# One image's latent scores earlier in TensorE's order, local values and gates sharing a bank, gates taken from the queries

## The reference

```
mod = silu(c) @ wmod                       # six rows of 128 per image: sa, ca, ga, sb, cb, gb
h   = layernorm(x) * (1 + ca) + sa
Q, K, V = h @ wq, h @ wk, h @ wv           # 16 heads of 8
local   = softmax(Q K / sqrt(8), windows of 32 tokens and the 32 before them) V
GQ, GK, GV = h @ wgq, pool(h @ wgk), pool(h @ wgv)     # 8 latent heads of 8, 64 latents, 4 tokens each
rem     = softmax(GQ GK / sqrt(8), causal over latents) GV @ r_out_w
gl, gr  = sigmoid(sum_d Q * gate_local_w), sigmoid(sum_d Q * gate_remote_w)   # one number per head
x = x + ga * ((gl * local + gr * rem) @ w_out)
h = layernorm(x) * (1 + cb) + sb
g = mean_s(relu(h @ gate_w1.T + gate_b1) @ gate_w2.T + gate_b2)               # 8 experts
x = x + gb * (gelu(h @ mW1.T + mb1) @ mW2.T + mb2)     # mW1 = W1 + sum_e g_e TW1_e, and so on
```

## Time and profile before

| what | value |
|---|---|
| median of three runs | 748.62 us |
| profiled execution | 748.97 us, span 747.20 us, granted TensorE clock 0.979 |
| busy share of the span | PE 86%, VectorE 72%, ScalarE 52%, GpSimd 39% |
| share of the chain that ended last | PE 42%, VectorE 26%, ScalarE 15%, issue 14% |
| one pass of the loop, `rden` to `rden` | 16.35 us, 28 passes |
| tanh of the gates in a pass | starts at 329.13, 0.58 us |

### The profile page before, as it was taken

The page is one execution under the profiler, slowest core; times in us unless marked ns, Lnnn a source line. Parts: engine busy times, 40 slices in busy tenths (PEclk is TensorE's granted clock), DMA queues, the critical chain, the costliest instruction groups (busy, mean ns, idle before and its releaser), DMA issues.

```text
span 747.2 us, 24120 instructions
## 1 busy us (share of the span) xinstructions
PE 645.6 (86%) x8822; PEld 506.4 (68%) x8822; DVE 538.1 (72%) x1241; ACT 384.9 (52%) x910; POOL 294.9 (39%) x415
## 2 busy tenths in 40 slices
PE   5588888788888878888887888888779999999998
PEld 3366666566666656666665666666558999898996
DVE  5568788888878888887888888788755546273552
ACT  2256655666665566666555666655543223423233
POOL 2256555455555545555554555555530000000000
PEclk9699999999999999999999999999978999999999
DMA  3757111000101100010110001010140010100101
GB/s 99 174 78 96 32 24 32 21 21 21 28 22 24 31 21 21 21 28 21 24 32 21 21 21 28 21 24 18 29 44 0 10 35 15 32 24 21 34 9 49
DMA packets 65797, 24.84 MB, mean 33 GB/s; under 512 B 38440, under 2 KB 64360, under 8 KB 65648
## 3 DMA queue, kind: packets, MB, share of 16 engines
q1 hardware_dynamic: 64320, 18.25, 10.2%
q0 software_dynamic: 1456, 6.31, 5.6%
HBM read 16.13 MB, written 8.40 MB: 33 GB/s over the span
## 4 chain that ended last, share of the span: by engine, by line
PE 42%; DVE 26%; ACT 15%; issue 14%; POOL 1%; ACTq 1%; DVEq 1%; DMA 0%; SPq 0%; POOLq 0%
DVE mx L561 10%; PE SB L820 7%; PE WB L808 7%; DVE rden L634 5%; ACT PT L443 5%; PE SB L927 5%; PE WB L795 4%; PE SB L795 4%; ACT xn_d L449 4%; DVE Pr L568 3%; ACT Pr L403 3%; PE SB L882 2%; PE SB L931 2%; ACT PL L435 2%; PE WB L970 2%
## 5 line engine op out<-in xcount | busy, mean ns | idle before, releaser
L336 POOL TENSOR_TENSOR KM<-K_ch,bd_scale 128x1024 f32<-128x1024 f32 x32 | 60.6, 1893 | 125.2 <-ACT K_ch L411 125.2
L634 DVE RECIPROCAL rden<-SB 128x256 f32<-128x256 f32 x32 | 56.2, 1758 | 54.5 <-PE SB L931 54.5
L506 ACT ACTIVATE Pr<-WB,mb1T 128x256 f32<-128x256 f32 x128 | 49.8, 477 | 75.7 <-PE WB L808 75.6
L561 DVE TENSOR_REDUCE mx<-SB 128x8 f32<-128x512 f32 x128 | 87.2, 681 | 1.5 <-PE SB L882 1.5
L403 ACT ACTIVATE Pr<-Pr 128x512 f32<-128x512 f32 x128 | 80.8, 631 | 10.8 <-DVE Pr L568 7.2
L568 DVE TENSOR_TENSOR Pr<-SB,mx 128x512 f32<-128x512 f32 x128 | 84.6, 681 | 0.0
L358 POOL TENSOR_TENSOR PT_sum<-PT 128x512 f32<-128x512 f32 x64 | 80.3, 1275 | 3.8 <-ACT PT L443 3.8
L443 ACT COPY PT<-SB 128x512 f32<-128x512 f32 x128 | 66.1, 622 | 0.0
L896 PE MATMUL SB<-ident,Pr 128*128 128x128 f32 x512 | 63.0, 276 | 0.9 <-ACT Pr L403 0.9
L820 PE MATMUL SB<-Pr,GA 128*128 128x256 f32 x256 | 61.2, 381 | 0.0
L835 PE MATMUL WB<-hT,wk 128*128 128x256 f32 x64 | 23.3, 448 | 43.2 <-DVE PlB L582 43.2
(11 more groups left out here) (195 smaller groups left out, 1518.5 us busy)
## 6 DMA issues: line engine op xcount, KB each, us to landing
x_all<-in_L_attn_x SPq DMA_DIRECT2D x32, 128.0 KB, 2.1
v_rows<-V_rows SPq DMA_DIRECT2D x32, 128.0 KB, 1.8
VBD<-v_rows SPq DMA_DIRECT2D x128, 32.0 KB, 1.8
TW<-in_L_ffn_TW POOLq DMA_DIRECT2D x16, 256.0 KB, 9.5
GA<-ga_rows POOLq DMA_DIRECT2D x1, 2048.0 KB, 10.5
out_x<-attT SPq DMA_DIRECT2D x16, 128.0 KB, 1.8
out_x<-y_ga SPq DMA_DIRECT2D x16, 128.0 KB, 1.8
PT<-in_L_ffn_W SPq DMA_DIRECT2D x2, 256.0 KB
```

What stands on the lines that cost most here:

```text
L336: nc.gpsimd.tensor_tensor(KM[:, :, W:KW], bc(K_ch[:], [P, 4, S], 1), bc(bd_scale[:], [P, 4, S], 2), ALU.mult).then_inc(km_ready, 1)
L561: nc.vector.tensor_reduce(mx[:, k, :], SB[k][:].rearrange("p (h j) -> p h j", h=8), AX.X, ALU.max).then_inc(mx_ready, 1)
L634: nc.vector.reciprocal(rden[:], SB[2][:, S:2 * S]).then_inc(rden_ready, 1)
```

## The change

Latent scores move from behind the first norm's transposes to in front of the second norm's (`latent_scores` ahead of L994). Local values and denominators go to `WB[2]`, the gates' bank, and wait until the tanh of the image before has read it. The remote product moves behind the first norm's transposes. Gates become a function of their own behind `scores`: `gate_w` times `QT`, into `WB[2]` once `a_loc` has read it; the copy `QT` waits for the last gates. VectorE takes both latent maxima and both subtractions in front of `rden`. GpSimd makes `GKBD` right behind `KM`. `gate_w` is made by VectorE alone, from the gate weights and the head pattern. The first expert group uses `WB[1]` in place of `WB[2]`.

```diff
@@ gpsimd step @@
                     nc.gpsimd.tensor_tensor(KM[:, :, W:KW], ...).then_inc(km_ready, 1)
+                    pool.wait_ge(gq_ready, 2 * (b + 1))
+                    nc.gpsimd.tensor_tensor(GKBD[0:NL], bc(GKT[:], [NL, LH, NL], 1),
+                                            bc(head[0:NL, 0:LH], [NL, LH, NL], 2), ALU.mult).then_inc(gkbd_ready, 1)
                 if has(it, 0):
                     inv_std(it, aggr_a, mv_a, ve_a, eps_a, rstd_a, rstd_a_s)
...
-                if has(it, 1):
-
-                    b = it - 1
-                    pool.wait_ge(gq_ready, 2 * (b + 1))
-                    nc.gpsimd.tensor_tensor(GKBD[0:NL], ...).then_inc(gkbd_ready, 1)
@@ scalar step @@
                     nc.scalar.copy(K_ch[:], WB[0][:, S:2 * S]).then_inc(k_ready, 1)
+                    at_least(act, gates_done, b)
                     nc.scalar.copy(QT[:], WB[0][:, 0:S]).then_inc(qt_ready, 1)
...
             def after(it):
-                if it == 0:
-                    act.wait_ge(wqT_done, 1)
-                    nc.scalar.copy(wqT, SB[1][:, 0:D]).then_inc(wqT_ready, 1)
-                    act.wait_ge(gate_w_done, 1)
-                    for k in range(2):
-                        nc.scalar.copy(gate_w[:, k, :]..., bc(SB[2][:, k * H:(k + 1) * H], [P, H, HD], 2)).then_inc(gate_w_ready, 1)
@@ vector step @@
                 if has(it, 3) and not tail:
                     output_times_ga(it - 3)
+                if has(it, 1):
+                    b = it - 1
+                    for t, pl, m in latent_tiles:
+                        latent_maximum(b, t, m)
+                    for tile in latent_tiles:
+                        latent_lowered(b, *tile)
                 if has(it, 2):
...
-                    nc.vector.reciprocal(rden[:], SB[2][:, S:2 * S]).then_inc(rden_ready, 1)
+                    nc.vector.reciprocal(rden[:], WB[2][:, S:2 * S]).then_inc(rden_ready, 1)
...
                 if has(it, 1):
                     b = it - 1
 
-                    for t, pl, m in latent_tiles:
-                        latent_maximum(b, t, m)
-                    latent_lowered(b, *latent_tiles[0])
                     maximum(b, 0)
-                    latent_lowered(b, *latent_tiles[1])
                     for k in range(4):
@@ vector after(0) @@
-                    then(nc.vector.tensor_tensor(gate_cols[:, 0:2 * H]..., bc(head[:], [P, 2, H], 1),
-                                                 bc(gate_col[:], [P, 2, H], 2), ALU.mult))
+                    for k in range(2):
+                        beside(nc.vector.tensor_tensor(gate_w[:, k, :]..., bc(head[:], [P, H, HD], 2),
+                                                       bc(gate_col[:, k:k + 1], [P, H, HD], 2), ALU.mult))
+                    dve.wait_ge(chain, n[0])
@@ tensor: projections, scores, values @@
-                bank_free(pe, it, (2, tg_ready, 1, 1))
...
-                for k in range(2):
-                    last = mm(WB[2][:, k * S:(k + 1) * S], gate_w[:, k, :], hT[:], start=True, stop=True)
-                last.then_inc(gates_done, 1)
...
-                bank_free(pe, it, (2, a_ready, 1, 1))
+                bank_free(pe, it, (2, pt_copied, 4, 3))
                 bank_free(pe, it, (2, pt_copied, 4, 4))
...
                 pe.wait_ge(vbd_loaded, N_VBD * (b + 1))
+                pe.wait_ge(tg_ready, b + 1)
...
-                            dst = SB[2][W * g:W * g + W, kb * W:kb * W + HALF].rearrange("p (k s) -> p k s", k=2)
+                            dst = WB[2][W * g:W * g + W, kb * W:kb * W + HALF].rearrange("p (k s) -> p k s", k=2)
...
+            def gates(it):
+
+                bank_free(pe, it, (2, a_ready, 1, 1))
+                if isinstance(it, int) and it == 1:
+                    pe.wait_ge(ga_ready, 1)
+                for k in range(2):
+                    last = mm(WB[2][:, k * S:(k + 1) * S], gate_w[:, k, :], QT[:], start=True, stop=True)
+                last.then_inc(gates_done, 1)
@@ tensor step @@
                     last.then_inc(y_done, 1)
+                if has(it, 1):
+                    latent_scores(it)
                 if has(it, 4):
                     pe.wait_ge(xn_d_s, T * (it - 4 + 1))
...
                     values(it)
-                    pe.wait_ge(remn_ready, it - 2 + 1)
-                    bank_free(pe, it, (3, yga_ready, 1, 1), (1, vrows_ready, 1, 1))
-                    for t in range(T):
-                        last = mm(WB[3][:, t * P:(t + 1) * P], r_out[:, t, :], rem_n[:], start=True, stop=True)
-                    last.then_inc(rem_done, 1)
...
                     last.then_inc(xT_done, 1)
-                if has(it, 1):
-                    latent_scores(it)
+                if has(it, 2):
+                    pe.wait_ge(remn_ready, it - 2 + 1)
+                    bank_free(pe, it, (3, yga_ready, 1, 1), (1, vrows_ready, 1, 1))
+                    for t in range(T):
+                        last = mm(WB[3][:, t * P:(t + 1) * P], r_out[:, t, :], rem_n[:], start=True, stop=True)
+                    last.then_inc(rem_done, 1)
+                if has(it, 1):
                     scores(it)
+                    gates(it)
...
             def after(it):
...
                     pe.wait_ge(attn_loaded, N_ATTN)
-                    nc.tensor.transpose(SB[1][:, 0:D], wq[:], ident[:]).then_inc(wqT_done, 1)
-                    pe.wait_ge(wqT_ready, 1)
-                    pe.wait_ge(attn_w_ready, 1)
-                    mm(SB[2][:, 0:2 * H], wqT, gate_cols[:, 0:2 * H], start=True, stop=True).then_inc(gate_w_done, 1)
```

More of the change, by code:

```diff
@@ L62, in adaln_block @@
         early = Pr[:].rearrange("p k n -> p (k n)").rearrange("p (k n) -> p k n", n=P)
-        tri, tri4, w_out, wqT, wv_in, gate_cols = (early[:, k, :] for k in range(6))
+        tri, tri4, w_out, wv_in = (early[:, k, :] for k in range(4))
         c_rows, silu_a, silu_b, silu_c, ga_sign, ga_abs = (early[0:B, k, :] for k in range(6, 12))
@@ L633, in step @@
                     dve.wait_ge(pv_done, b + 2)
-                    nc.vector.reciprocal(rden[:], SB[2][:, S:2 * S]).then_inc(rden_ready, 1)
+                    nc.vector.reciprocal(rden[:], WB[2][:, S:2 * S]).then_inc(rden_ready, 1)
                     dve.wait_ge(rden_ready, b + 1)
-                    nc.vector.tensor_tensor(a_loc[:], SB[2][:, 0:S], rden[:], ALU.mult).then_inc(a_ready, 1)
+                    nc.vector.tensor_tensor(a_loc[:], WB[2][:, 0:S], rden[:], ALU.mult).then_inc(a_ready, 1)
                 if has(it, 0):
@@ L681, in experts @@
                 dve.wait_ge(g_done, done + 1)
-                nc.vector.tensor_scalar(gT[:, cols], WB[2][0:E, 0:n_b] if g0 == 0 else SB[0][0:E, 0:n_b], 1.0 / S,
+                nc.vector.tensor_scalar(gT[:, cols], WB[1][0:E, 0:n_b] if g0 == 0 else SB[0][0:E, 0:n_b], 1.0 / S,
                                         gate_b2[:], ALU.mult, ALU.add).then_inc(g_ready, 1)
                 dve.wait_ge(g_done, done + 2)
-                rows, biases = (WB[2], SB[3]) if g0 == 0 else (SB[1], SB[2])
+                rows, biases = (WB[1], SB[3]) if g0 == 0 else (SB[1], SB[2])
                 for g in range(g0, g1):
@@ L707, in after @@
                                                wv_in[:].rearrange("p (g h d) -> p g h d", g=G, h=4)))
-                    then(nc.vector.tensor_tensor(gate_cols[:, 0:2 * H].rearrange("p (k h) -> p k h", k=2), bc(head[:], [P, 2, H], 1),
-                                                 bc(gate_col[:], [P, 2, H], 2), ALU.mult))
+                    for k in range(2):
+                        beside(nc.vector.tensor_tensor(gate_w[:, k, :].rearrange("p (h d) -> p h d", d=HD), bc(head[:], [P, H, HD], 2),
+                                                       bc(gate_col[:, k:k + 1], [P, H, HD], 2), ALU.mult))
+                    dve.wait_ge(chain, n[0])
                     nc.vector.tensor_scalar(w_out_half[:], w_out[:], 0.5, None, ALU.mult).then_inc(attn_w_ready, 1)
@@ L848, in projections @@
                 last.then_inc(v_done, 1)
-                bank_free(pe, it, (2, tg_ready, 1, 1))
-                if isinstance(it, int) and it == 1:
-                    pe.wait_ge(ga_ready, 1)
-                    pe.wait_ge(gate_w_ready, 2)
-                for k in range(2):
-                    last = mm(WB[2][:, k * S:(k + 1) * S], gate_w[:, k, :], hT[:], start=True, stop=True)
-                last.then_inc(gates_done, 1)
             def scores(it):
@@ L930, in values @@
                 for g in range(G):
-                    last = mm(SB[2][W * g:W * g + W, S:2 * S], ones_bd[:], PT_sum[:, g, :], start=False, stop=True,
+                    last = mm(WB[2][W * g:W * g + W, S:2 * S], ones_bd[:], PT_sum[:, g, :], start=False, stop=True,
                               skip_group_check=True)
@@ L1028, in experts @@
                 pe.wait_ge(hid_summed, g1 * GB)
-                bank = WB[2] if g0 == 0 else SB[0]
+                bank = WB[1] if g0 == 0 else SB[0]
```

(1 more changed line is left out.)

14 lines of the change are left out of this document (5 added, 9 removed).

## The result

The changed kernel takes 754.38 us (median of 8 runs, 751.67 to 756.18) against 748.71 (8 runs, 747.49 to 749.38) on the same chip: ratio 1.0074, 95% interval 1.0054 to 1.0093. It is slower, by 5.67 us in the medians; the forecast was 756.0, range 747.0 to 761.0. The profiled execution took 755.03 us, 6.06 more than that of before, span 753.3, granted clock 0.982.

What follows compares the result with a forecast made beforehand. A ring of waits through three engines was taken to bound the kernel: +0.25 us per pass, 28 passes +7.0, setup and ends +0.4, on 748.97 makes 756.4, less 0.35 for the median: forecast 756.0 us, range 747.0 to 761.0.

Steps and rivals of the forecast that it cites:

- the ring: Chain of waits through TensorE, VectorE and ScalarE, once per image, said to bound the kernel; 16.35 us per pass before.
- wait for `GVBD`: TensorE ahead of the latent scores: they start 0.14 us after `GVBD` ends and frees their bank.
- hold of the latent scores: Latent scores hold TensorE 1.40 us ahead of the second norm's transposes, a wait new on the ring.
- transposes: TensorE, from the second norm's transposes to the local values: 0.31 us, where the row before has 0.37.
- `hT` to scores: TensorE works off further waits after `hT` before the first score matmul: 0.24 us, lower end 0.04.
- VectorE's wait there: VectorE, free at 327.47, waits 0.65 us for the scores ahead of the first score maximum.
- VectorE's pause ahead of `rden`: VectorE's pause of 1.75 us takes the latent maxima and subtractions, hidden there, and shrinks to 0.4 us.
- setup and ends: Work outside the loop's 28 passes, with passes 2 and 3 gaining about 0.15 each: +0.4 us, between -1.0 and +2.0.
- Scores not held up: Rival at the first score matmul: VectorE goes straight on to maximum 0; faster, 737.8 us; chance 0.13.
- A wash: Rival: wait behind `hT` 0.04 and half the first-matmul cost, so nothing per pass, 749.0 us; chance 0.13.
- Held statistics: Rival: `GKBD` on GpSimd holds VectorE's batch statistics, 0.6 us more per pass, about 773 us; chance 0.04.
- Gates behind the scores: Gates done about 1.1 us after the scores; tanh ends ahead of the first exponential's input, hidden with about 0.1 us spare.

Runs made afterwards that it cites:

- f1: Changed kernel with the latent scores written to `SB[3]` and `SB[2]`, so they no longer wait for `GVBD`; pass 15.71 us, median 730.09 us, ratio 0.9761.
- f2: e1 with the scores' wait for the relu put behind their other waits; pass 16.01 us, median 742.11 us, ratio 0.9912.
- e2: Changed kernel with latent scores and VectorE's order back in their old places, gates and banks staying moved; pass 16.30 us, median 746.50 us, ratio 0.9984.
- e1: Changed kernel with the first norm's transposes ahead of the latent scores and `hT` behind `xn_d`; pass 16.23 us, median 748.46 us, ratio 0.9984.
- g1: f1 plus hidden layer in `WB[1]`, first norm's transposes ahead of the latent scores, `hT` behind `xn_d`; pass 15.07 us, median 714.79 us, ratio 0.9557.
- g2: g1 with the weights of experts 4 and 5 loaded in step 32, not step 3; pass 15.07 us, median 709.67 us, ratio 0.9476.

## Why the prediction was right

**The mechanism.** Both claims held: the latent scores came onto the ring through the wait for `GVBD` (f1 takes it away: -0.81 a pass), and the scores then waited for hidden layer, relu and `hT` (f2: -0.51). Neither alone makes the loss: with either one taken away the pass is shorter than before the change (15.71 and 16.01 against 16.35).

**The terms**, predicted and measured in the pass whose `GVBD` starts at 323.83:

| term | predicted us | measured us |
|---|---|---|
| wait for `GVBD` | 0.14 | 0.15 (324.11 to 324.26) |
| hold of the latent scores | 1.40 | 1.36 |
| transposes | 0.31 | 0.32 |
| values to `rden` | 1.69 | 1.69 |
| values to hidden layer | 1.56 | 1.57 |
| hidden layer to relu | 0.81 | 0.81 |
| relu to the end of `hT` | 1.02 | 1.03 |
| `hT` to scores | 0.24 | 0.20 |
| scores to maximum | 1.89 | 1.85 |
| VectorE's wait there | 0.65 | 0.56 |

`rden` came 1.44 later behind `GVBD` (1.46), and the first maximum 0.68 sooner behind `rden` (0.62). The pass: +0.25 predicted, +0.17 measured; the 0.08 is made of three terms that were 0.04 too long and four that were 0.01 too short, no single one. VectorE's pause ahead of `rden` was 0.19 and not 0.4. From the start of the latent scores to the end of `PlB` it took 3.18 (324.26 to 326.76 + 0.68) and not 2.99, chiefly since the second tile was complete 1.53 behind that start, not 1.46, and since `PlB` ahead of a pause lasts its whole 0.68, not the 0.60 to the next row's start. That is off the ring.

**The sum.** 28 passes gave 4.64 us for 7.0 predicted; setup and ends 1.42 for 0.4. The errors went against each other, so the time, 754.38 for 756.0, is better than its terms. The mis-sized second term has two parts. I had steps 2 and 3 gain 0.15 each. The spacing of `GVBD` from step 3 to step 4 did gain 0.19 (15.69 against 15.88), but that from step 2 to step 3 lost 0.69 (15.59 against 14.90). The prediction carried the ring of the loop over to step 2. That step has no second norm, so in the kernel before TensorE did not wait for `xn_d`: its values ran ahead of `GVBD`, which starts at 44.44.
```profile
43.18 1.21 PE L927 MATMUL SB<-PT,VBD 128*32 128x64 f32 x64
...
45.51 1.76 DVE L634 RECIPROCAL rden<-SB 128x256 f32<-128x256 f32 x1 [0.79 <-PE SB L931]
...
55.27 0.48 DVE L546 BATCH_NORM_STATS2 st_a<-x_all 128x6 f32<-128x128 f32 x2
```
In the changed kernel the latent scores stand in front of them and wait for `GVBD`, which starts at 44.81.
```profile
45.23 1.53 PE L967 MATMUL WB<-GKBD,GQT 128*128 128x256 f32 x4 [1.56 <-DVE GVBD L615]
...
46.69 1.20 PE L915 MATMUL WB<-PT,VBD 128*32 128x64 f32 x64
...
48.40 1.76 DVE L631 RECIPROCAL rden<-WB 128x256 f32<-128x256 f32 x1
...
56.30 0.47 DVE L537 BATCH_NORM_STATS2 st_a<-x_all 128x6 f32<-128x128 f32 x2
```
So `rden` comes 3.59 behind `GVBD` in place of 1.07, 2.52 later and not 1.46; less the 1.87 that VectorE gives away, that is 0.65 of the 0.69. GpSimd's weight loads, which in that step come later too and stand in front of `KM`, are not the cause: VectorE's statistics, which stand ahead of all that it takes from GpSimd there, are already 1.03 late (56.30 against 55.27), and `GVBD` of step 3 is 1.06 late, 0.03 more.

The other part is the way out of the loop, 0.52, for which the prediction had no term. Up to the first expert group's `gT` the lag falls from 5.51 to 4.58 (559.72 against 555.14), and up to the next `y_ga` it rises to 6.05 (563.89 against 557.84). TensorE's products between the two ran at a granted clock of 0.50 (from 559.90 to 563.90; the lower level, 1.2 GHz), in the kernel before at 0.87 (from 555.30 to 557.80); in both TensorE had stood idle ahead of them, 2.07 and 2.02 us. This is read from the traces; no run separates it.

**The rivals.** Scores not held up: refuted by the row of L858. A wash: the wait behind `hT` was 0.20, not 0.04. Held statistics: nil. They run beside `GKBD` at their usual length:
```profile
336.14 1.04 POOL L339 TENSOR_TENSOR GKBD<-GKT,head 64x512 f32<-64x512 f32 x1
336.19 0.47 DVE L537 BATCH_NORM_STATS2 st_a<-x_all 128x6 f32 x2
```
so the rule of the Trainium skill ("SBUF — State Buffer", Who interferes with whom) that was cited for this holds here. Gates behind the scores: tanh starts at 332.51, and the first exponential, at 333.32, still waits 0.21 for VectorE and not for tanh; e2 shows for the gates' whole part that it costs nothing.

## What to carry to other kernels

When work is moved into an engine's pause, look for what its output bank waits for: here VectorE's pause was 1.75 us long, but TensorE's part of the moved work wrote to a bank that is freed late, and `rden` came 1.44 us later; with two banks that the same change had emptied it comes 0.64 later (f1, 3.00 against 2.36). What the moved work used to cover comes to light too: list what the next instruction waits for, and make each of these early before the cover goes. Look at the first steps by themselves: work that falls into a pause in the loop may meet none there. And try the wait that ends last at the end of a list of waits.

## What the runs showed of the hardware that was not expected

Waits that are already met are not always free when they stand behind the one that ends last: two of them cost TensorE 0.20 us (e1 against f2), and 0.22 a pass is some 6 us over 28. Beside heavy weight transfers in the first pass of a loop TensorE stopped for 2.2 to 3.6 us in seven kernels with nothing in the profile but "issue", and behind the 3.48 of g1 it ran at the lower clock; issuing a quarter of the transfers later took 5.1 us off (g2 against g1). In e2, 8 of 12 runs lie at 745.6 to 746.7 us and 4 at 750.8 to 752.0, as if the stop came in some executions only; the profiled one, 750.91, has it. Why the changed kernel, with the same transfers, shows none stays open.
